# Values of four key tiles in one burst: a two-layer attention and expert kernel on one NeuronCore

## The reference, cut to what matters

```python
q, k, v = proj(query), proj(key), proj(value)            # 2 batches, 16 heads, 8 columns per head
scores = jnp.einsum('bhqd,bhkd->bhqk', q, k) / np.sqrt(DK)
scores = jnp.where(mask == 0, -1e9, scores)              # block 0 only
attn = jax.nn.softmax(scores, axis=-1)
x = jnp.einsum('bhqk,bhkd->bhqd', attn, v)               # "values" below
...
x = x + L0_xattn(layernorm(x), ctx);  x = x + L0_ffn(layernorm(x))
x = x + L1_xattn(layernorm(x), ctx);  x = x + L1_ffn(layernorm(x))
```

## Time and profile before

| | us |
|---|---|
| median of 3 runs | 256.22 (256.07 to 256.94) |
| profiled execution, its own time | 256.07 |
| its span in the trace | 254.2 |
| loop 0, steps 14 to 26 | 44.3 to 69.5 |
| loop 1, steps 14 to 26 | 160.9 to 180.9 |

### The profile page before, as it was taken

The page is one execution under the profiler, slowest core; times in us unless marked ns, Lnnn a source line. Parts: engine busy times, 40 slices in busy tenths (PEclk is TensorE's granted clock), DMA queues, the critical chain, the costliest instruction groups (busy, mean ns, idle before and its releaser), DMA issues.

```text
span 254.2 us, 5091 instructions
## 1 busy us (share of the span) xinstructions
PE 224.8 (88%) x1644; PEld 137.0 (54%) x1656; DVE 186.6 (73%) x578; ACT 155.4 (61%) x225; POOL 79.5 (31%) x228
## 2 busy tenths in 40 slices
PE   3879899999999999989898789999988989989870
PEld 1464444445444448977686444455444447767760
DVE  7779876777676385678657897888775657789864
ACT  6775897565964762342223458777766674796570
POOL 4571346365522100100201153444412043344421
PEclk9999999999999999999999999999999999999999
DMA  6878799900110028800042683300000000000000
GB/s 212 275 214 173 208 137 182 339 26 26 40 62 3 0 62 161 152 3 0 0 124 65 217 280 96 95 4 0 4 0 3 0 0 4 1 0 3 0 21 22
DMA packets 18180, 20.41 MB, mean 80 GB/s; under 512 B 1553, under 2 KB 15609, under 8 KB 17825
## 3 DMA queue, kind: packets, MB, share of 16 engines
q1 hardware_dynamic: 17578, 19.16, 29.0%
q10 hardware_dynamic: 576, 0.94, 1.2%
HBM read 15.90 MB, written 4.19 MB: 79 GB/s over the span
## 4 chain that ended last, share of the span: by engine, by line
PE 57%; DVE 22%; issue 8%; DMA 4%; ACT 3%; POOL 2%; SPq 1%; DVEq 1%; POOLq 0%; ACTq 0%
PE bank L376 11%; PE bank L451 10%; PE bank L429 9%; PE bank L425 4%; DVE st L1061 4%; PE bank L549 3%; PE bank L550 3%; PE bank L569 3%; DVE row_max L875 3%; PE bank L624 2%; ACT q_stack L1370 2%; PE bank L382 2%; DVE shared_area L1099 2%; DMA aw<-in_attn_w 1%; PE bank L589 1%
## 5 line engine op out<-in xcount | busy, mean ns | idle before, releaser
L1385 ACT ACTIVATE probs<-bank 128x1024 f32<-128x1024 f32 x64 | 64.3, 1023 | 14.1 <-PE bank L429 9.0
L872 DVE CUSTOM_DVE_ANT_0 discard<-bank,bias_q 128x512 bf16<-128x512 f32 x64 | 43.3, 690 | 17.0 <-PE bank L376 15.3
L376 PE MATMUL bank<-k_stack,q_stack 72*128 72x512 bf16 x128 | 48.4, 384 | 4.1 <-DVE row_max L875 1.5
L875 DVE TENSOR_REDUCE row_max<-bank 128x1 f32<-128x512 f32 x64 | 42.0, 687 | 9.2 <-PE bank L376 6.7
L429 PE MATMUL bank<-q_stack,k_stack 102*128 102x256 bf16 x256 | 43.7, 272 | 1.1 <-ACT probs L1385 0.3
L451 PE MATMUL bank<-probs,v_ext 128*32 128x256 f32 x512 | 40.3, 391 | 0.2 <-ACT o_sb L1392 0.2
L1370 ACT COPY q_stack<-bank 6x512 bf16<-6x512 bf16 x32 | 18.5, 577 | 27.0 <-PE bank L398 26.9
L429 PEld LDWEIGHTS bank<-q_stack,k_stack 102*128 102x128 bf16 x256 | 24.8, 98 | 17.1 <-issue 1.4
L1626 POOL CAST max_part<-row_max 128x4 bf16<-128x4 f32 x32 | 6.2, 194 | 78.2 <-DVE row_max L875 44.4
L376 PEld LDWEIGHTS bank<-k_stack,q_stack 72*128 72x128 bf16 x128 | 12.3, 96 | 27.2 <-issue 11.9
L1433 ACT ACTIVATE early<-bank 128x512 f32<-128x512 f32 x12 | 7.1, 595 | 23.2 <-PE bank L550 23.2
(11 more groups left out here) (191 smaller groups left out, 362.5 us busy)
## 6 DMA issues: line engine op xcount, KB each, us to landing
k_stack<-k_bounce SPq DMA_DIRECT2D x9, 384.0 KB
q_bounce<-q_part SPq DMA_DIRECT2D x12, 192.0 KB, 3.0
k_bounce<-early SPq DMA_DIRECT2D x4, 384.0 KB, 3.0
experts_w<-in_wu SPq DMA_DIRECT2D x1, 1024.0 KB, 4.8
early<-in_wu SPq DMA_DIRECT2D x1, 1024.0 KB, 7.0
experts_w<-in_wg SPq DMA_DIRECT2D x1, 816.0 KB, 13.2
experts_w<-in_wu SPq DMA_DIRECT2D x1, 816.0 KB, 15.5
experts_w<-in_wd SPq DMA_DIRECT2D x1, 768.0 KB, 16.2
```

The source lines that it names most:

```text
L376: mm(bank[:, qt, :], q_stack[0:STACK, b, h, qt * 128:(qt + 1) * 128], k_stack[0:STACK, b, h, :], start=True, stop=True).then_inc(for_max, 1)
L872: ins = dve.tensor_tensor_reduce(discard[:, qt, :], bank[:, qt, :], bias_q[:, qt, :], 1.0, LOWEST, ALU.add, ALU.max, o)
L875: ins = dve.tensor_reduce(o, bank[:, qt, :], AX.X, ALU.max)
L1385: act.activation(probs[:, n % (2 * HG), :], bank[:, at:at + 2, :].rearrange("p a n -> p (a n)"), ACT.Exp, scale=SCALE).then_inc(exp_done, 1)
```

## The change

In both loops:

- the four key tiles of a group's values stand in one step, 9+4g ("group step" below), one behind the other, at the end of the step; the steps between have none;
- o_copy of the group stands in the same step on ACT;
- o_transpose of the group stands in step 13+4g, directly ahead of the next group's values, and no longer in an even step of its own;
- in the group steps from 13 on, the transposes of the maxima stand behind the first rows, ahead of the columns, where they were the last of the step;
- the divide stands on DVE in step 13+4g, behind both maxima of the step.

No instruction is added or taken away.

```diff
--- before.py
+++ after.py
@@ -48,6 +48,8 @@
 FIRST_LAGS = (3, 3, 4, 4)
 PV_LAG = LAG + HG
 HEADS = B * H
+OUT_COPY_STEP = (PV_LAG, PV_LAG)
+OUT_TURN_STEP = (PV_LAG + 4, PV_LAG + 4)
 LAST_WINDOW = B * E1 // 2 - 1
 BOTH_ON_ACT = (2, 5)
 
@@ -286,6 +288,10 @@
 
             return m + (FIRST_LAGS[m] if m < len(FIRST_LAGS) else LAG)
 
+        def group_of(s, first):
+
+            return (s - first) // HG if s >= first and (s - first) % HG == 0 else None
+
         head_of_step = [{column_step(l, m): m for m in range(HEADS)} for l in range(2)]
 
         SHARED = T0 // 2
@@ -635,6 +641,7 @@
                     n, columns = l * HEADS + s, s in head_of_step[l]
                     m = l * HEADS + head_of_step[l].get(s, 0)
                     transposes = s % MG == 1 and 0 <= (s - 3) // MG < HEADS // MG
+                    soon = group_of(s, OUT_TURN_STEP[l]) in range(B * NG - 1) and transposes
                     at_once = columns and m == n - MG - 1
                     rows = l * BEGUN <= s < HEADS
                     if rows:
@@ -645,6 +652,8 @@
                         max_transpose(l * HEADS // MG + (s - 3) // MG)
                         score_rows(n, 1)
                         keep_busy(5, 2 if s == FIRST_LAGS[0] else 0)
+                    if soon:
+                        max_transpose(l * HEADS // MG + (s - 3) // MG)
                     if columns:
                         score_cols(m, range(0, KT // 2))
                         score_cols(m, range(KT // 2, KT))
@@ -652,12 +661,13 @@
                         score_rows(n, 1)
                     if l == 0 and s < FIRST_LAGS[0]:
                         keep_busy(5, 2)
-                    if transposes and not at_once:
+                    if transposes and not at_once and not soon:
                         max_transpose(l * HEADS // MG + (s - 3) // MG)
-                    if s % HG == (PV_LAG + 1) % HG and s >= PV_LAG + HG:
-                        o_transpose(l * B * NG + (s - PV_LAG) // HG - 1)
-                    if s >= PV_LAG:
-                        values(l * B * NG + (s - PV_LAG) // HG, (s - PV_LAG) % HG)
+                    if group_of(s, OUT_TURN_STEP[l]) in range(B * NG - 1):
+                        o_transpose(l * B * NG + group_of(s, OUT_TURN_STEP[l]))
+                    if group_of(s, PV_LAG) in range(B * NG):
+                        for kt in range(KT):
+                            values(l * B * NG + group_of(s, PV_LAG), kt)
                     for at, f in extra:
                         if at == s:
                             f()
@@ -1123,8 +1133,6 @@
 
                 for s in range(HEADS + PV_LAG):
                     n = l * HEADS + s
-                    if s % HG == (PV_LAG + 2) % HG and s > PV_LAG + HG:
-                        divide(l * B * NG + (s - PV_LAG) // HG - 1)
                     if l * BEGUN <= s < HEADS:
                         head_max(n, 0)
                     for at, f in extra:
@@ -1132,6 +1140,8 @@
                             f()
                     if l * BEGUN <= s < HEADS:
                         head_max(n, 1)
+                    if group_of(s, OUT_TURN_STEP[l]) in range(B * NG - 1):
+                        divide(l * B * NG + group_of(s, OUT_TURN_STEP[l]))
                     for at, f in extra:
                         if at == s:
                             f()
@@ -1414,8 +1424,8 @@
                         max_copy(l * HEADS // MG + (s - 3) // MG)
                     if s in head_of_step[l]:
                         exponentials(l * HEADS + head_of_step[l][s])
-                    if s % HG == (PV_LAG - 1) % HG and s >= PV_LAG:
-                        o_copy(l * B * NG + (s - PV_LAG) // HG)
+                    if group_of(s, OUT_COPY_STEP[l]) in range(B * NG):
+                        o_copy(l * B * NG + group_of(s, OUT_COPY_STEP[l]))
                     for at, f in extra:
                         if at == s:
                             f()
```

## The result

The changed kernel takes 273.31 us (median of four, 271.05 to 275.82) beside 256.58 us for the kernel before (four runs, 256.07 to 258.74). It is slower by 6.1%; the ratio is 1.0607, with a 95% interval of 1.0543 to 1.0672. The profiled execution took 271.05 us, 15.0 more than the profiled one of before (256.07); its span is 269.3 against 254.2. The forecast was 264.2 with a range from 258.0 to 267.0: the direction was right, the size much too small.

A forecast was written before the change was run, and what follows sets the result against it. PE, busy 88% of the span, was taken as the bound; the burst saves it 0.69 us a group, but waits for MISC, DVE and POOL cost more: +0.6 in loop 0, +7.5 in loop 1 on 256.07, 264.2 us, range 258.0 to 267.0.

The forecast's parts named there:

- Rival 1: Both loops: PE stays the bound and the burst gains, 246 us, or 248 to 250 with DVE's pace; chance 0.10.
- Rival 2: Both loops: the waits are there but weaker, as ACT's copy gets in earlier; 258 us; chance 0.14.
- rival 3: Whole kernel: gain and loss cancel, or waits fall between the burst's tiles; within 0.3% of 256.2 us; chance 0.03.
- Rival 4: Behind loop 1: late logits delay second-layer experts and ACT's normalisation stands behind the last burst; 266 to 268 us; chance 0.13.
- the sum: Whole kernel: +0.6 us for loop 0 and +7.5 for loop 1, +8.1 on 256.07, giving 264.2 us.
- The 1.27 us of a cycle in loop 1: Loop 1, each cycle of four steps: forecast to take 7.91 us against 6.64, 1.27 longer.

The follow-up runs named there:

- e3: Changed kernel with o_transpose a step later, divide at that step's head and transposes of the maxima last in their step; 265.32 us, ratio 1.035.
- e8: Changed kernel with ACT's sel_cast moved from step 24 to step 26; 271.46 us, ratio 1.0572.
- e6: Changed kernel's group-step order, but one key tile of values in each step as in the kernel before, o_copy in step 12+4g; 262.47 us, ratio 1.022.
- e10: Changed kernel with DVE's maxima of loop 1 over 256 of the 512 keys only; 271.48 us in one execution, loop 1 cycle 7.86 us.
- e5: Changed kernel with ACT's copy of a group step's maxima one place earlier, ahead of the exponential of the step before; 269.98 us, ratio 1.0533.
- e11: Kernel before with the key tiles of values two and two in loop 0 only; 254.8 us, ratio 0.9917.
- e1: Changed kernel with loop 1 put back as in the kernel before, so the burst in loop 0 only; 260.85 us, ratio 1.0156.
- e7: Changed kernel with three extra matmuls ahead of each o_transpose of loop 1 but the last; 271.59 us, ratio 1.059.
- e15: Changed kernel with the burst in loop 0 only, loop 1 as before, and sel_cast in step 26; 260.24 us, ratio 1.0129.
- e12: Changed kernel with three extra matmuls ahead of each o_transpose of loop 1, one in loop 0, and sel_cast in step 26; 271.02 us, ratio 1.0549.
- e13: e6 with one more copy of the maxima on ACT, ahead of the one PE waits for, in loop 1's seven group steps; 265.46 us, ratio 1.0311.
- e2: Changed kernel with loop 0 put back as in the kernel before, so the burst in loop 1 only; 268.66 us, ratio 1.0456.
- e4: Changed kernel with the group step's transposes of the maxima behind the burst instead of ahead of the columns; 272.62 us, ratio 1.0615.
- e9: e3 with DVE's maxima of loop 1 over 256 of the 512 keys only; 258.38 us in one execution, loop 1 cycle 7.14 us.
- e14: Kernel before with the key tiles of values two and two in both loops; 257.41 us, ratio 1.0009.

## Why the prediction was wrong in size

**Right.** The waits are where the forecast put them, and the kernel is slower for the reason given: a burst that saves PE 0.69 us and waits that cost more. Step by step: burst 1.87 to the next piece (forecast 1.86); idle time ahead of the o_transpose 0.75 in loop 1 and 0.31 in loop 0 (0.84 and 0.4); PE's share down; DVE idle 1.72 us once in four steps. In loop 0, +1.6 by step 14 (+1.4), +1.0 from step 26 to the logits (+0.7), -2.1 from there to the exit (-2.0). In loop 1, relative to its entry, +1.0 at the end of step 9 (+1.0) and +3.0 at step 14 (+2.9). Rival 1, in which PE stays the bound, fell with the changed kernel and again with e3: even with the wait for ACT's copy away, loop 1 takes 7.42, 1.5 above the 5.95 of PE alone, where the rival gave DVE at most 0.5. Rival 2 fell with the waits, rival 3 with the total. Rival 4 had the right side and the wrong place: between the first statistics, +15.4, and the end, +15.1, nothing more was lost, and the median lies above its 268 too.

**What was missing or wrong, in the order of size.** The step that failed is the sum: it had no term for the clock and none for sel_cast, and one link of ACT's chain too short. The forecast lacked 6.9 us of the profiled execution, which is the fastest of the four, and 9.1 of the median.

1. *The clock, an estimated 3.6 to 4.9 us.* The sum was made at the full clock throughout, as in the slices of before, and had no term for it. In the changed kernel step 22 to 26 of loop 1 takes 9.71 us, not 8.06: 1.65. In the second fall the burst at 208.90 alone is 1.70 longer, and the o_transpose ahead of it takes 0.59 to its values (208.31 to 208.90) for 0.34. For a PE that works all the time a stretch of 4 us at 0.70 costs 1.2 us and one at 0.50 costs 2.0, so 204 to 212 is worth 3.2 at most. Step 26 to the logits took 4.3 us more than before, 2.7 beyond the forecast's 1.6, which fits; but that stretch has waits too that the forecast may have had wrong, and they were not told apart. Repeats go the same way: 271.05 us at a mean clock of 0.977, 273.31 and 273.32 at 0.971 and 0.972, 275.82 at 0.959.
2. *sel_cast, 1.5 us.* "ACT gets to that copy only behind two exponentials" is true of every group step but that of step 25, where ACT's extra of step 24 stands there too. The list of the changed wait's queue was read from one cycle of loop 1; loop 0's extras were not gone through. e8 shows the term from step 22 to 26, and e6 that it comes with the order.
3. *A link of the chain, 0.8 us.* I had the copy 0.92 behind the second exponential's start, as exponentials follow each other. It is 1.04: with 1.94 from 177.28, the second starts at 178.20, ends at 179.22 and the copy starts at 179.24. A copy of the maxima starts behind the end of the exponential, while the next exponential starts 0.1 ahead of it. That is 0.12 of the 0.14 to 0.15 by which both cycles are longer than forecast, six times; the rest is the o_transpose, 0.34 and not 0.31 to its values.

**Nearly right in sum, wrong in its split.** The 1.27 us of a cycle in loop 1 were 0.84 for MISC and 1.1 for DVE, less 0.69. e10 leaves out about 2 us of DVE's work in a cycle and gets 0.20 back, e5 takes the copy ahead of the exponential and gets nothing. In the changed kernel the cycle is ACT's chain with the burst in it, link by link from the rows of ACT and PE above: 0.87 from the rows behind the burst to the exponential at 175.03, 1.50 to the copy at 176.53 (that link waits for PE, and PE's rows for DVE), 0.75, 0.92 and 1.04 to the copy at 179.24, 0.77 to the o_transpose, 0.34 and 1.87 for the burst: 8.06. ACT has nothing to do for most of the burst (1.33 of 1.87 us), and by this chain that, more than the bank MISC, is what it costs. This is read from the chain and from e5 and e10, which leave the cycle nearly as it is; no run made ACT's own work less, so it is not shown by an experiment. The rule of the Trainium skill that rival 1 was set beside ("TensorEngine Tiling (Array Packing)", Key Properties: a change of the tiling mode drains the engine) would make the change a gain, and for PE by itself the trace agrees: 1.87 us for a burst of four, and 0.44 of the expected 0.46 us a cycle in e11. What decided the time was what the other engines do meanwhile, of which that rule does not speak.

**Open.** What brings the clock down. In the profiled executions it falls at varying places: in loop 0 in e1, e7, e8, e10 and e15, at 152 to 154 us in e12 and e13, between steps 10 and 14 of loop 1 in e2, e4, e8, e10 and e12, only behind step 26 of it in e3, e5 and e9. Behind that step it falls in every kernel with bursts of four in loop 1. In those of e6, e11 and e14, without such bursts, it does not fall in the loops; in that of e13, the longest execution of five, it does, also behind step 26. Over all executions the mean clock is 0.953 to 0.992 in kernels with bursts of four in loop 1 and 0.977 to 0.999 in the others, the kernel before included, whose lowest is 0.981 (259.69 us); the one at 0.66 in e11 stands apart. So the fall goes with bursts of four (in e1 and e15 it is in loop 0, where theirs are), but the two ranges overlap, and why it does was not found: e13 does not show that waits are enough, e15 moved the longest wait and did not remove it, and e12 filled the waits ahead of the o_transposes and the clock fell all the same.

## What to carry to other kernels

Bunching work on the engine that sets the pace saves its switches, but starves those that it feeds. Here it paid only where the others had time in hand: two tiles in loop 0, where a step of PE is 2.1 us and two maxima 1.22, gave 0.44 of 0.46 us a cycle; two in loop 1, with a step of 1.66, lost 0.32, and four lost in both. When a wait moves in front of an engine's queue, list everything that stands between the two in every pass of the loop, extras included, and ask whether the engine waited for is behind by its order or by its amount of work: only the first can be mended by a swap. When an extra is moved out of the way of one wait, look at what it stands ahead of next: sel_cast gave back 0.9 of its 1.5 us. And give the clock a term or a range of its own: here the sum at the full clock came out some 4 us short by it.

## What the runs showed of the hardware

- An exponential of 128x1024 (1.02 us) is followed by the next after 0.92 us, but by a copy of 6x512 only after 1.04 to 1.05 (the trace of the changed kernel).
- The granted clock of TensorE fell to its lower level in a cycle in which no wait of PE was longer than 0.75 us (the changed kernel, 0.57 in 188 to 192 us), and sixteen value matmuls then took 3.57 us for 1.94. It stayed full behind a wait of 1.71 us (e12, at 75.83).
- Executions of one kernel differ with the mean clock: the changed one takes 271.05 us at 0.977 and 273.32 at 0.972, the one of e13 264.13 at 0.999 and 265.31 to 265.92 at 0.987.
